# Attention in groups of four units: one V product per group, five buffers of transposed probabilities, new engine orders, a wider GpSimd addition

## The reference

```python
q = (x @ Wq + bq).reshape(B, S, N_HEAD, HEAD_DIM).transpose(0, 2, 1, 3)   # B 2, S 2048, 16 heads of 32
...
scores = jnp.einsum('bhqd,bhkd->bhqk', q / math.sqrt(HEAD_DIM), k)
scores = scores + attention_bias                                         # (2, 16, 2048, 2048) fp32
scores = jnp.where(src_mask, -jnp.inf, scores.astype(jnp.float32))
probs = jax.nn.softmax(scores, axis=-1).astype(v.dtype)
ctx = jnp.einsum('bhqk,bhkd->bhqd', probs, v)
ctx = ctx.transpose(0, 2, 1, 3).reshape(B, S, D)
x = x + (ctx @ Wo + bo)
```

## Time and profile before

| what | value |
| --- | --- |
| median of three runs | 3619.0 us |
| profiled execution | 3623.18 us, its span 3621.4 us |
| PE, PEld busy | 3559.3 us (98%), 2451.5 us (68%) |
| DVE, ACT, POOL busy | 2256.5, 2184.5, 2062.6 us |
| POOL addition L1196 | x509, 1827.8 us, mean 3634 ns |
| ACT exponential L1286 | x512, mean 2002 ns |
| PE transposes L1232 | x8192, 1024.9 us busy |
| bias loads | x512, 1024 KB each, median 7.0 us from issue to landing |
| TensorE clock granted, 1000 to 1300 us | 1.00 |

### The profile page before, as it was taken

How to read it: one execution, slowest core, us unless ns; L and a number is a source line. 1 busy time by engine, 2 the same in 40 slices (tenths; PEclk the granted TensorE clock), 3 DMA queues, 4 the chain that set the end, 5 groups by cost and what they waited for, 6 DMA issues and landing times. The chain is left out here.

```text
span 3621.4 us, 79854 instructions
## 1 busy us (share of the span) xinstructions
PE 3559.3 (98%) x32051; PEld 2451.5 (68%) x32051; DVE 2256.5 (62%) x4503; ACT 2184.5 (60%) x3047; POOL 2062.6 (57%) x782
## 2 busy tenths in 40 slices
PE   7999999999999999999999999999999999999998
PEld 3444468888888888888888888887544444444444
DVE  7676668888888888888888888887211111111102
ACT  2343369999999999999999999998210210110110
POOL 1111169898899989899998899996310110120100
PEclk8999999999999999999999999999999999999999
DMA  5555598888998888988888988887300110111002
GB/s 190 202 186 185 189 394 326 320 332 322 349 371 322 322 321 331 379 339 325 321 321 335 387 330 321 322 320 262 139 24 11 35 35 11 40 55 39 20 24 93
DMA packets 210118, 828.62 MB, mean 229 GB/s; under 512 B 25044, under 2 KB 58964, under 8 KB 134488
## 3 DMA queue, kind: packets, MB, share of 16 engines
q1 hardware_dynamic: 204532, 815.09, 59.7%
q10 hardware_dynamic: 5220, 8.42, 0.6%
HBM read 732.19 MB, written 91.23 MB: 227 GB/s over the span
## 5 line engine op out<-in xcount | busy, mean ns | idle before, releaser
L1196 POOL TENSOR_TENSOR at_tiles<-at_tiles,at_negmask 128x1792 f32<-128x1792 f32 x509 | 1827.8, 3634 | 191.9 <-DMA at_tiles<-in_bias 178.8
L1286 ACT ACTIVATE at_tiles<-at_tiles,at_rmin 128x2048 f32<-128x2048 f32 x512 | 1025.3, 2002 | 58.2 <-DVE at_rmin L1333 57.6
L1232 PE MATMUL at_ps_p<-consts,at_tiles 128*128 128x128 f32 x8192 | 1024.9, 272 | 0.1
L1232 PEld LDWEIGHTS at_ps_p<-consts,at_tiles 128*128 128x128 f32 x8192 | 929.8, 141 | 37.8 <-ACT at_prob_t L1294 0.6
L1294 ACT ACTIVATE at_prob_t<-at_ps_p 128x512 f32<-128x512 f32 x1536 | 831.5, 596 | 128.7 <-PE at_ps_p L1232 127.1
L1333 DVE CUSTOM_DVE_ANT_0 at_tiles<-at_ps_s,at_tiles 128x1024 f32<-128x1024 f32 x512 | 624.7, 1220 | 119.2 <-PE at_ps_s L1213 112.4
L1213 PE MATMUL at_ps_s<-at_k_stack,at_q_stack 128*128 128x512 f32 x2048 | 677.4, 432 | 6.0 <-DVE at_rmin L1333 4.1
L1333 DVE CUSTOM_DVE_ANT_0 at_tiles<-at_ps_s,at_tiles,at_rmin 128x1024 f32<-128x1024 f32 x512 | 657.8, 1285 | 18.8 <-PE at_ps_s L1219 0.5
L1249 PE MATMUL at_ps_c<-at_prob_t,at_v 128*32 128x128 f32 x16384 | 500.3, 274 | 0.6 <-DVE at_ctx_rows L1351 0.6
L1249 PEld LDWEIGHTS at_ps_c<-at_prob_t,at_v 128*32 128x32 f32 x16384 | 431.6, 110 | 43.7 <-issue 43.0
L1710 PE MATMUL ff_ps_m<-ff_w,ff_hid 128*128 128x512 f32 x1024 | 441.8, 593 | 0.0
(11 more groups left out here) (193 smaller groups left out, 2635.3 us busy)
## 6 DMA issues: line engine op xcount, KB each, us to landing
at_tiles<-in_bias SPq DMA_DIRECT2D x512, 1024.0 KB, 7.0
at_k_stack<-k_hi SPq DMA_DIRECT2D x128, 256.0 KB, 5.1
at_k_stack<-k_lo SPq DMA_DIRECT2D x128, 256.0 KB, 5.3
negm<-em_mask_out SPq DMA_DIRECT2D x32, 512.0 KB, 6.6
at_q_stack<-q_hi SPq DMA_DIRECT2D x128, 128.0 KB, 5.1
at_q_stack<-q_lo SPq DMA_DIRECT2D x128, 128.0 KB, 5.2
at_v<-v SPq DMA_DIRECT2D x64, 256.0 KB, 7.8
at_negmask<-negm SPq DMA_DIRECT2D x32, 512.0 KB, 9.7
```

The source lines that it names most:

```text
L1196: pool.tensor_tensor(tiles[s][:, 0:PCOLS], tiles[s][:, 0:PCOLS], negm[s][:, 0:PCOLS], ALU.add).then_inc(s_pool, 1)
L1232: last = pe.transpose(ps_p[k][:, y * P:(y + 1) * P], tiles[s][:, t * P:(t + 1) * P], ident)
L1286: act.activation(tiles[s][:, :], tiles[s][:, :], ACT.Exp, bias=rmin[:, s, 1:2], scale=-1.0, accum_out=rsum[:, s:s + 1]).then_inc(s_exp, 1)
```

## The change

Units go in groups of four (`GROUP`, `NG` = 128) rather than in pairs.

- `pv(g)` multiplies V for four units in one go, 128 instructions, and `parts` and `context` handle four units at once (a copy of 128 x 256, a scaling of 128 x 128). `parts_sum` is two products for four units.
- `p_t` is five buffers of one unit instead of two of a pair. A copy for unit `u` waits for the V product of the group of `u - 5`. The fifth is allotted behind the second K, Q, V buffers, and `exp_w` moves into the embed stage's region.
- `pool_columns` is 1920 rather than 1792, so TensorE's mask product has 128 columns rather than 256.
- TensorE, ScalarE and VectorE get new orders over `g`, with `u = 4g`. The score products run three to four units ahead of the transposes, and `pv(g - 1)` stands between the second half of `qk(u + 3)` and the first of `qk(u + 4)`.
- `cx_all` holds eight heads' columns rather than sixteen. `store(g)` writes four tiles of it after every eighth head, in runs of 1 KB of memory; there are 16 such stores of 512 KB, as before. It is issued by ScalarE at the end of its turn `g + 2`. `context` waits for the store before it overwrites a buffer.
- `rsum` has sixteen columns rather than eight.

```diff
-    at.pool_columns = S - 256
+    at.pool_columns = S - 128
...
-    at.p_t = [sb(f"at_prob_t{i}", [P, 2, S // P, P]) for i in range(2)]
+    at.p_t = [sb(f"at_prob_t{i}", [P, S // P, P]) for i in range(4)]
...
+    at.p_t.append(sb("at_prob_t4", [P, S // P, P]))
+    at.cx_sb = sb("at_ctx_parts", [P, 2 * P])
+    at.cx_all = sb("at_ctx_rows", [P, RING, D // 2])
...
+            def pv(g):
...
+                after(pe, s_cxo, g)
+                if g * GROUP % RING == 0:
+                    pe.wait_ge(s_vin[n % 2], 16 * (n // 2 + 1))
+                for c in range(CH - TB, CH):
+                    k, i = bank(GROUP * g + GROUP - 1, c)
+                    pe.wait_ge(s_pe[k], i + 1)
+                for pair in range(2):
+                    for i in range(QUART):
+                        for q in range(4):
+                            half, j = divmod(q, 2)
+                            t = half * QUART + i
+                            probs = p_t[(GROUP * g + 2 * pair + j) % SLOTS]
+                            last = pe.matmul(ps_c[q * HD:(q + 1) * HD, pair * P:(pair + 1) * P], v_sb[n % 2][:, t, :],
+                                             probs[:, t, :], start=(i == 0), stop=(i == QUART - 1))
...
+            for g in range(-1, NG + 1):
+                u = GROUP * g
+                qk(u + 3, 0)
+                transposes(u, (0, 1, 2))
+                qk(u + 3, 1)
+                pv(g - 1)
+                qk(u + 4, 0)
+                transposes(u, (3,))
+                transposes(u + 1, (0,))
+                qk(u + 4, 1)
+                transposes(u + 1, (1, 2, 3))
+                qk(u + 5, 0)
+                parts_sum(g - 1)
+                transposes(u + 2, (0, 1))
+                qk(u + 5, 1)
+                transposes(u + 2, (2,))
+                qk(u + 6, 0)
+                transposes(u + 2, (3,))
+                transposes(u + 3, (0,))
+                qk(u + 6, 1)
+                transposes(u + 3, (1, 2, 3))
...
+            def take(u, c):          # ScalarE, and the same wait on VectorE
...
+                if u >= SLOTS:
+                    act.wait_ge(s_pv, (u - SLOTS) // GROUP + 1)
...
+            def store(g):
+                n = g * GROUP // RING
+                if not 0 <= g < NG or n % HALF_HEADS != HALF_HEADS - 1:
+                    return
+                act.wait_ge(s_cxo, g + 1)
...
+                to = cxv[n // HEADS][:, of, half * D // 2:(half + 1) * D // 2]
+                act.dma_start(to, cx_all[:, of, :]).then_inc(s_st[i], 16)
+
+            for g in range(-1, NG + 2):                       # ScalarE
+                u = GROUP * g
+                take(u + 1, 0)
+                take(u + 1, 1)
+                take(u + 1, 2)
+                take(u + 1, 3)
+                exp(u + 4)
+                take(u + 2, 1)
+                take(u + 2, 2)
+                take(u + 2, 3)
+                take(u + 3, 0)
+                take(u + 3, 2)
+                take(u + 3, 3)
+                exp(u + 5)
+                take(u + 4, 1)
+                exp(u + 6)
+                exp(u + 7)
+                take(u + 4, 3)
+                store(g - 2)
...
+                after(dve, s_st[s // GROUP], 16 * (n // HALF_HEADS))      # in context(g)
...
+            for g in range(-2, NG + 1):                       # VectorE
+                u = GROUP * g
+                parts(g - 1)
+                scores(u + 4, 1)
+                scores(u + 5, 0)
+                take(u + 2, 0)
+                scores(u + 5, 1)
+                scores(u + 6, 0)
+                take(u + 3, 1)
+                scores(u + 6, 1)
+                context(g - 1)
+                scores(u + 7, 0)
+                take(u + 4, 0)
+                scores(u + 7, 1)
+                take(u + 4, 2)
+                scores(u + 8, 0)
```

More of the change, by code:

```diff
@@ L998, in attention_buffers @@
     RING = 8
+    GROUP = 4
     SPAN = RING * P
@@ L1068, in attention_stage @@
     RING = 8
-    PCOLS = S - 256
+    PCOLS = net.at.pool_columns
     HALF = S // 2
@@ L1074, in attention_stage @@
     NU = NH * RING
-    NP = NU // 2
+    GROUP = 4
+    NG = NU // GROUP
+    SLOTS = GROUP + 1
+    HALF_HEADS = HEADS // 2
     KT = S // P
@@ L1113, in attention_stage @@
         s_rv = sem("at_rinv_ready")
-        s_st = [sem(f"at_ctx_stored{i}") for i in range(RING // 2)]
+        s_st = [sem(f"at_ctx_stored{i}") for i in range(RING // GROUP)]
         def bank(u, c):
@@ L1143, in load_v @@
                 _, _, b, qh, h = place(n * RING)
-                after(sp, s_pv, 4 * (n - 1))
+                after(sp, s_pv, RING // GROUP * (n - 1))
                 at.read_v(sp, n % 2, b, h)
@@ L1154, in load_ffn @@
             def load_ffn():
-                for i in range(2):
-                    sp.wait_ge(s_st[i], 16)
-                    sp.wait_ge(s_st[i + 2], 16)
+                for stored in s_st:
+                    sp.wait_ge(stored, 2 * 16)
                 sp.dma_start(net.cx[:], net.ctx.rearrange("(t j p) d -> t p j d", j=TJ, p=P)[0]).then_inc(net.s_cx, 16)
@@ L1204, in qk @@
             def qk(u, a):
+                if not 0 <= u < NU:
+                    return
                 n, s, b, qh, h = place(u)
@@ L1233, in transposes @@
                     last.then_inc(s_pt[k], 1)
[L1235 to L1239, removed]
-                    pe.wait_ge(s_vin[n % 2], 16 * (n // 2 + 1))
[L1241 to L1250, removed]
-                last.then_inc(s_pv, 1)
@@ L1253, in parts_sum @@
[L1253 to L1277, removed]
+            def pv(g):
+                if not 0 <= g < NG:
+                    return
+                n = g * GROUP // RING
+                after(pe, s_cxo, g)
+                if g * GROUP % RING == 0:
+                    pe.wait_ge(s_vin[n % 2], 16 * (n // 2 + 1))
+                for c in range(CH - TB, CH):
[9 more added lines that the diff above has]
+                                             probs[:, t, :], start=(i == 0), stop=(i == QUART - 1))
+                last.then_inc(s_pv, 1)
@@ new lines, in parts_sum @@
+            def parts_sum(g):
+                if not 0 <= g < NG:
+                    return
+                pe.wait_ge(s_cxs, g + 1)
+                for pair in range(2):
+                    o = 2 * P + pair * 2 * HD
+                    last = pe.matmul(ps_c[:, o:o + 2 * HD], cx_sb[:, pair * P:(pair + 1) * P], stack, start=True, stop=True)
+                last.then_inc(s_cxm, 1)
+            for g in range(-1, NG + 1):
[19 more added lines that the diff above has]
+                transposes(u + 3, (1, 2, 3))
@@ L1290, in take @@
                 k, i = bank(u, c)
-                pr, j = divmod(u, 2)
-                after(act, s_pv, pr - 1)
+                if u >= SLOTS:
+                    act.wait_ge(s_pv, (u - SLOTS) // GROUP + 1)
                 act.wait_ge(s_pt[k], i + 1)
-                act.activation(p_t[pr % 2][:, j, 4 * c:4 * c + 4, :].rearrange("p t q -> p (t q)"), ps_p[k][:],
+                act.activation(p_t[u % SLOTS][:, 4 * c:4 * c + 4, :].rearrange("p t q -> p (t q)"), ps_p[k][:],
                                ACT.Copy).then_inc(s_pe[k], 1)
[L1297 to L1319, removed]
+            def store(g):
+                n = g * GROUP // RING
+                if not 0 <= g < NG or n % HALF_HEADS != HALF_HEADS - 1:
+                    return
+                act.wait_ge(s_cxo, g + 1)
+                i = g % (RING // GROUP)
+                of = slice(GROUP * i, GROUP * (i + 1))
+                half = n // HALF_HEADS % 2
+                to = cxv[n // HEADS][:, of, half * D // 2:(half + 1) * D // 2]
+                act.dma_start(to, cx_all[:, of, :]).then_inc(s_st[i], 16)
@@ L1321, in _ @@
+            for stored in s_st:
+                act.wait_ge(stored, 2 * 16 * B * QH)
         @block.vector
@@ L1337, in take @@
             def take(u, c):
+                if not 0 <= u < NU:
+                    return
                 k, i = bank(u, c)
-                pr, j = divmod(u, 2)
-                after(dve, s_pv, pr - 1)
+                if u >= SLOTS:
+                    dve.wait_ge(s_pv, (u - SLOTS) // GROUP + 1)
                 dve.wait_ge(s_pt[k], i + 1)
-                v.tensor_copy(p_t[pr % 2][:, j, 4 * c:4 * c + 4, :].rearrange("p t q -> p (t q)"),
+                v.tensor_copy(p_t[u % SLOTS][:, 4 * c:4 * c + 4, :].rearrange("p t q -> p (t q)"),
@@ L1343, in take @@
                               ps_p[k][:]).then_inc(s_pe[k], 1)
[L1345 to L1378, removed]
+            def parts(g):
+                if not 0 <= g < NG:
+                    return
+                dve.wait_ge(s_pv, g + 1)
+                v.tensor_copy(cx_sb[:], ps_c[:, 0:2 * P]).then_inc(s_cxs, 1)
@@ new lines, in context @@
+            def context(g):
+                if not 0 <= g < NG:
+                    return
+                n, s, b, qh, h = place(GROUP * g)
+                r = GROUP * g % (2 * RING)
```

(9 more changed lines are left out.)

15 lines of the change are left out of this document (8 added, 7 removed).

## The result

The changed kernel takes 3629.1 us in the median (3626.2 to 3636.9) against 3619.65 us for the kernel before: a ratio of 1.003, 95% interval 1.0019 to 1.0041. The forecast was 3639 and slower. Its profiled execution has a span of 3626.9 us.

What follows compares the result with a forecast made beforehand. TensorE's order of work in attention was taken as the bound. For the profiled execution, 3623.2 - 38 (V once per group) + 3 (GpSimd) + 55 (stores) = 3643 us; against the median 3639, range 3588 to 3672.

Steps and rivals of the forecast that it cites:

- What bounds the kernel: In attention, the order of work on TensorE sets the time: 15.87 us for four units; GpSimd is second.
- V once per group: On TensorE, a group of four units takes 15.57 us against 15.87: 38 us less, bounds 15 and 43.
- The mask product: On TensorE, 128 mask columns instead of 256 gain between 0 and 31 us; no gain was taken.
- rival 3: TensorE's mask product does shrink: its group is 15.33, GpSimd's 15.36 decides, 64 us less, stores' 55 more: 3610; chance 0.12.
- GpSimd: Adding 1920 columns takes GpSimd 30.7 us a head, just under TensorE; costed at 3 us, bounds 0 and 64.
- The orders of the engines: In attention, VectorE and ScalarE keep up with TensorE's new order; nothing charged, 0.1 us of cover at the tightest place.
- The store: Context stores have 9.0 us of room but land after 10.5 to 15.8, holding up VectorE, then TensorE: 55 us, bounds 0 and 75.
- Turns of the DMA engines: Store and bias load pieces alternate one for one, so 16 more pieces per engine add up to 5.6 us.

Runs made afterwards that it cites:

- the early store: The changed kernel with ScalarE issuing the store of a group's context one turn sooner, store(g - 1) instead of store(g - 2): 3591.8 us, ratio 0.9914.
- The experiment with pieces of 4 KB: The changed kernel, store still late but written as 128 pieces of 4 KB instead of 512 of 1 KB, context rows in another order: 3591.7 us, ratio 0.9918.

## Why the prediction held, and where it didn't

- *What bounds the kernel.* Right. TensorE is busy throughout in quiet heads before and after, and each shortening of the mask product moved the time, though not by its full size.
- *V once per group.* Predicted 15.57 us a group with no gain from the mask. The kernel with the new orders and 256 columns has 30.91 us a head, 15.46 a group: 52 us of TensorE's time gained by grouping, not 38 (of which the early store with these columns shows 23 us in the end, since the unnamed waits and the mask reloads come on top). The term was mis-sized, the transposes above all: with 256 columns the seven runs take 6.44 us a group, where I used 6.64 (runs of eight take 0.80, not 0.84, the run of four 0.36, not 0.40). Plain score products are 0.06 cheaper in all, V and the sums of parts 0.14 dearer (3.63 and 0.39, not 3.58 and 0.30), and the product with the switch in took the 0.76 that I used.
- *The mask product.* The failed step. I took the end "nothing", from the 64-column row, and gave the full 31 us as the other end; 27 us of TensorE's time was right, 0.12 to 0.07 us. The row I leaned on is a product of another kind: the 0.11 us behind the sum of parts didn't carry over. That also decides rival 3: its quiet head (15.33 a group) was right, but its time (3610) left out the terms below, as the forecast did.
- *GpSimd.* I had 15.36 us a group, and an addition every 3.83 us makes 15.32 (the 61 us are full), yet it was costed at 3 us where 13 were measured. "Stays just under TensorE" was true of a TensorE at 15.57 only; at 15.26 GpSimd is the slower one and its lead shrinks.
- *The orders of the engines.* Right: TensorE waits for neither VectorE nor ScalarE in the quiet heads, and VectorE was ready for the buffer 9.3 us after the issue in most places, where I had 9.0.
- *The store.* The mechanism was right in place, in the pieces and in who waits for whom: 12 waits of 14. The size was too large. I had 55 us, without the clock. Measured are 31 us of TensorE's wait, about 39 with the clock's part, and about 40 by experiment. The split was wrong: first stores in heads without mask reload were to land after 10.5 us and took 14.7 to 16.2; second ones 14.2 and took 10.6 to 11.6; with reload 15.8 and took 8.4 to 12.6. I had averaged the DMA engines, and the slowest one decides; why the stores at the mask reloads landed sooner than I had is open.
- *Turns of the DMA engines.* That the pieces alternate one for one I read from equal counts, and turns of ten pieces on each side would give the same counts, and about the same landing: the reading was right, its evidence wasn't enough. The series of pieces 0.348 us apart show it. "DMA: Bandwidth & Descriptors" in the Trainium skill, "Queues, rings and completion order", has packets of 9 to 17 descriptors per turn; the series don't agree, there a turn is one piece. The experiment with pieces of 4 KB doesn't tell the two apart.
- *Missing.* Neither the clock after a stall (11 us) nor TensorE's unnamed waits, by inference for instruction loads (21 us), had a term. The forecast for the profiled execution was 3643, it took 3629. Unseen gains of 41 us (27 mask, 14 grouping) and 24 us by which the store was too dear (55 - 31) stand against unseen losses of 42 us (11 clock, 21 unnamed waits, 10 GpSimd): that makes 23 us less, where it was 14 less, so some 9 us have no name. That the time came so near was partly luck: errors of both signs, each larger than the miss, cancelled.

## What to carry to other kernels

When a buffer is reused sooner, write down for each transfer how many microseconds lie between its issue and the next use, and issue it as soon as its data is there; here moving one line by a turn turned a change that lost about 10 us into one that gains 29. Count a transfer's pieces, not its bytes, when another queue keeps the DMA engines busy, and take the slowest engine. Price a stall of TensorE above its length where the rows show the clock falling behind it, and keep a second engine's share clearly below the first's.

## What the runs showed of the hardware

- Where TensorE stood still for 5.1 to 5.9 us at a store its granted clock was 1.2 GHz for 6.8 us (three places), and for 3.4 us at three more, where it had stood still for 2.0 to 4.6 us. Not each such stop has it: one of 3.0 us at 1538 us and one of 2.3 us at 1261 us kept 2.4 GHz. The kernel before kept 2.4 GHz from 500 to 2480 us, and the one with the early store fell twice for 3.4 us, at stops of 1.8 us.
- TensorE's unnamed waits all end 2.2 to 2.6 us after a 16 KB load of instructions began: 17 waits, 21 us, nine of them in the last 17 of 128 V instructions. With blocks of 64 there were 14 such waits, 8 us, and with blocks of 128 but a mask product of 256 columns 17, 12.6 us. In the kernel before there was none. How far ahead the loads are asked for isn't seen.
- Two queues with work for the same DMA engine took turns piece by piece, 1 KB of the store and 8 KB of the load in 0.348 us (1290.8 to 1292.7 us in the changed kernel).
- A product of 128 x 128 bf16 columns is followed by a transpose after 0.067 us, one of 256 after 0.120; but before the sum of parts the same saving is given back in the sum (0.29 us for both in either kernel).
